# Value products of a two-layer transformer kernel in three groups of four sets a turn instead of six of two

## The chip, the cores and the metric

The kernel runs on one core of a Trainium2 chip. The metric is the device time of one execution in microseconds (us). The core has a tensor engine (PE; its weight loads are listed apart as PEld), a vector engine (DVE), a scalar engine (ACT), GpSimd (POOL) and SyncE (SP), which issues the DMAs. Each runs its own list of instructions in order, and they wait for each other by semaphores.

## The reference

Two transformer layers, each with attention and a feed-forward part on the same normalized input, over a batch of 2 sequences of 1024 rows and 512 columns, all in float32. Cut to what matters here:

```python
x = L0_attn_X                                  # (2, 1024, 512)
xn = _layernorm(x, axis=-1)
x = x + _L0_attn_ref(xn, ...) + _L0_ffn_ref(xn, ...)
xn = _layernorm(x, axis=-1)
x = x + _L1_attn_ref(xn, ...) + _L1_ffn_ref(xn, ...)

# attention: 16 heads of 32 columns, rotary embedding, causal mask
scores = jnp.einsum('bhqd,bhkd->bhqk', Qr, Kr) * DH ** (-0.5)
scores = jnp.where(causal, jnp.finfo(scores.dtype).min, scores)
pattern = jax.nn.softmax(scores, axis=-1)
heads = jnp.einsum('bhqk,bhkd->bqhd', pattern, Vh).reshape(b, t, d)
return heads @ Wo.T

# feed-forward: hidden 2048 in layer 0, 1408 in layer 1 (there with scales for rows)
gated = jax.nn.silu(gate) * up
return jnp.einsum('bsh,dh->bsd', gated, w_down)
```

## The kernel before

The program is one list of steps, `STEPS`, made by Python functions before anything is emitted. Every engine walks the whole list and emits its own part of each step, so the list sets the order on all five engines at once. There are four parts of it: two sequences times two layers (`layer(b, l)`, by `plan` and `paced`).

A part has four **turns**, one for each group of four heads. A turn consists of

- 32 **natural** steps (`nat`): scores in natural order, in which the vector engine finds the row maxima and the scalar engine sums exponentials, to get the logarithm of each softmax denominator (`guess`, `better`, `log`, `flip` put it into rows of `QS`);
- 12 **sets** of the transposed scores (`SETS`; 4 for the first half of the query rows, 8 for the second), each of four `st` steps, one a head: a matmul of up to 512 columns into one of three PSUM banks (`SS` two, `OE` one), and an exponential by the scalar engine into the tile `pr`, from which the value product reads. In the sets on the diagonal (0 to 3 and 8 to 11) GpSimd masks a block (`causal`) when the four exponentials are done;
- the **value products** (`pv`), one a set: for each of the four heads a matmul whose stationary operand is 32 columns of `val` and which writes its own 32 partitions of the bank `O` (half of `OE`). Four heads thus take four strips of 32 columns of the array;
- `heads` (the scalar engine copies `O` to `ah`, the vector engine makes the rest `al`), then four output products (`wo`, three matmuls each) that the vector engine adds to `xres`;
- at the end the next turn's four **projections** (`proj`, 12 matmuls each), merged with the output products of this turn by `merge`.

`pr` holds the weights of `RING` = 4 sets. The first exponential of set i waits for the value product of set i - 4 (semaphore `p_pv`, in `st_` of the scalar engine). The same tile holds the rotary halves of the projections (`parts`, `swapped`), so the vector engine's part of a projection must come behind the value products that read there.

`weighted` places the value products before: behind the last `st` of sets 2, 4, 6, 8 and 10 the two sets (i - 2, i - 1), and sets 10 and 11 at the end of the turn, where `merge` puts them between the first and the second projection.

The feed-forward part is cut in pieces of four matmuls (`G` gate, `U` up; three pieces each a chunk and half) and the down products (`D`), and these are the filling: `PACE` has one digit for each item of the attention, the number of pieces that come before it, and `LATER` delays the weight splits (`w`: the scalar engine rounds a weight to its high part, for instance `wdh`, GpSimd makes the low part). For the down weights of layer 1 GpSimd first multiplies `raw` by `ds`, and the scalar engine's cast waits for that.

All large products are three matmuls of rounded halves (high x high, high x low, low x high); the value products are plain float32, which the engine runs in two passes, so one listed instruction appears as two matmuls in the trace.

Of the kernel before, what the change touches and what calls it, by code (L numbers as in the profile page):

```python
# [52 lines left out]
SETS = [(c, kb) for c in range(NC) for kb in range(TPC * (c + 1))]  # L53
RING = 4
# [58 lines left out]
def diagonal(i):  # L113

    c, kb = SETS[i]
    return kb >= TPC * c


def weighted():

    out = []
    for i, (c, kb) in enumerate(SETS):
        out += [[("st", i, h)] for h in range(HG)]
        if diagonal(i):
            out[-1].append(("causal", i))
        for at, step in ((0, "guess"), (2, "better"), (3, "log"), (5, "flip")):
            if i == at // 2:
                out[2 * (at % 2 - 2) + 1].append((step, 1))
        if i and i % 2 == 0:
            out.append([("pv", i - 2), ("pv", i - 1)] + [("heads", SETS[i - 1][0])] * (SETS[i - 1][0] != c))  # L130
        if i == 6:
            out += output(0)
    return out
# [17 lines left out]
def projections():  # L151

    proj = [[("proj", t, False)] + [("rotate", t - 1)] * (t > 0) for t in range(2 * NC)]
    proj.append([("rotate", 2 * NC - 1)])
    return proj


def output(c):

    return [[("wo", c, i), ("add_wo", c, i)] for i in range(TPC)]  # L160
# [11 lines left out]
def turn(g, more):  # L172


    out = [[("turn", g)]]
    if more:
        out.append([("w", "A")])
    out += natural() + weighted()
    if g == NG - 1:
        return out  # L180
    n = len(SETS)
    last = [[("pv", n - 2), ("pv", n - 1), ("heads", 1)]]
    return out + merge(projections(), last + output(1))


def merge(proj, rest):

    return [proj[0], rest[0], proj[1]] + rest[1:3] + proj[2:4] + rest[3:] + proj[4:]


def plan(b, l):


    final = (b, l) == (B - 1, 1)
    gates, downs = mlp(l)
    pieces, late = in_order(gates[:-1], downs[:-1])
    items = []
    for g in range(NG):
        items += turn(g, not (final and g == NG - 1))
    if not final:  # L200
        items[items.index([("turn", NG - 1)])].insert(0, ("v_load", 1 - l))
    n = len(SETS)
    items.append([("pv", n - 2), ("pv", n - 1), ("heads", 1)] + [("v_weights", 1 - l)] * (not final))
    items += output(1)
    if l == 1 and not final:
        halves = [k for k, it in enumerate(items) if ("pv", TPC * 2 - 1) in it]
        items[halves[-1]].append(("x_next", 0))
        items[-TPC - 1].append(("x_next", 1))
        for rt in range(TPC):
            items[rt - TPC].append(("row", 0, rt))  # L210
        items[-1] += normal(0)

    (g0, g1), (d0, d1) = gates[-1], downs[-1]
    if final:
        g0[-1] = [x for x in g0[-1] if x[0] != "w"]
        g1, d1 = ([[x for x in p if x[0] != "w"] for p in q] for q in (g1, d1))
    pieces += g0[:3] + late + g0[3:] + g1[:3]
    if l == 0:
        rows = [piece + [("row", 1, rt)] for rt, piece in enumerate(d0)]
        rows[-1] += normal(1)  # L220
        pieces += rows + g1[3:] + early(1) + [piece + [("row", 1, TPC + i)] for i, piece in enumerate(d1)]
        items += norms(1, range(TPC))
    else:
        for c, d in enumerate((d0, d1)):
            for i, piece in enumerate(d):
                piece.append(("store", c * TPC + i))
        pieces += d0 + g1[3:9]
        if not final:
            items += norms(0, range(TPC))
            pieces[-1].append(("keep", 0))  # L230
        pieces += g1[9:] + (early(0) if not final else []) + d1
    first = opening(l)
    if (b, l) != (0, 0):
        first = [x for x in first if [x] not in early(l)]
    else:
        first.insert(first.index(("rotate", 1)) + 1, ("first",))
        first.append(("second",))
    return first, items, pieces
# [7 lines left out]
def normal(layer):  # L246

    return [("stats", layer, 0), ("xn", layer, 0), ("xn", layer, 1)]


def layer(b, l):

    first, items, pieces = plan(b, l)
    return loads(first + paced(items, pieces, PACE[b][l], LATER[b][l]))

# [13 lines left out]
def opening(layer):  # L269
# [13 lines left out]

PACE = (
    (
        ("30010030010010010003030201121212022010111001000101100100000101000001000010100000010200000100000000101",
         "00000210010100102003020311132121112010011021000000010100101101000000000100100000011010000201000000110",
         "30000101000101010112121211120212121021010100100000201000001001000001001001010000010011000000000000100",
         "040001011002010110130302020212120210200100110000010100200101010000010000101000000100100000117037j040"),
        ("01002201010101021022053203121111111020002001000000100000000000000000000000000000000000000000000000003",  # L290
         "00000021000101010113021212111113020210020101000001001000000100100002000000100000000000000000000000022",
         "00100011010001020112030303021112121030100101000002001000000101000000000000000000000000000000000000010",
         "0101000200000200011210202011101101010101000000000010000000000000000000000000000000000000000010015040"),
    ),
    (
        ("40001110100001100203020311121203111011010100200000200100000103000000000010100000100100000010000000012",
         "00000110101010013102101111211121111020120001000010010102001001000000000100100001002100000100000000011",
         "30000111000101010103120322021121212021001001000000100100000101000001000010100000010120000010000000001",
         "003000110110100210130302021112120220100101110000020010001010010000010000100100000100100001018027j220"),
        ("13001111000100110302050311210121111100100001000100100200001001000000000000000000000000000000000000001",  # L300
         "10200011000100101013122112111112210210021001000000100100000100100000000010010000000000000000000000201",
         "00100210020101010112030302120212121020111001000001000000000101000000000000000000000000000000000000030",
         "0000111000102000102111430301010100000000000000000000000000000000000000000000000000000000000d000"),
    ),
)
LATER = (("04410342c042070023000200", "111ic009o00023l200"),
         ("0090030dk0201f4011000200", "511400087042265"))
STEPS = START + [x for b in range(B) for l in (0, 1) for x in [("begin", b, l)] + layer(b, l)]


# [867 lines left out]
```

## Time and profile before

| | |
|---|---|
| median of 3 runs | 1912.29 us (1911.0 to 1917.44) |
| profiled execution, its own time | 1915.39 us |
| its span | 1913.7 us |
| mean granted TensorE clock | 0.988 |
| PE busy | 1806.6 us, 94% |
| ACT busy | 1091.3 us, 57% |
| DVE busy | 1049.8 us, 55% |
| POOL busy | 721.5 us, 38% |

The span is the time from the first to the last instruction of the profiled execution. A busy share is an average over stretches with different limits: the tensor engine's matmuls are pipelined, each is listed for longer (0.39 us for 512 columns) than it keeps the next one away (0.23 us), so its busy time says that something was in the array, and the starts of neighbouring matmuls say what each really costs.

### The profile page before, as it was taken

The numbers are of one execution on the slowest core, as the hardware profiler recorded it, in microseconds if no ns is written. First come the engines' busy times: TensorE is split into PE (matmuls) and PEld (weight loads), VectorE is DVE, ScalarE is ACT, GpSimd is POOL, SyncE is SP. The second block draws the span as 40 slices with busy tenths as digits, with TensorE's granted clock in tenths as the row PEclk, the third lists the DMA queues.
The fourth block names the chain that finished last, engine by engine and source line by source line (L and its number), as shares of the span: only waits on it lengthen the run. The fifth ranks groups of instructions, "written<-read, shape, count | busy, mean of one in ns | idle before, by whom it ended". The sixth has DMA issues, their size and how long they took to land.

```text
span 1913.7 us, 24678 instructions
## 1 busy us (share of the span) xinstructions
PE 1806.6 (94%) x8656; PEld 1328.4 (69%) x8656; DVE 1049.8 (55%) x2368; ACT 1091.3 (57%) x2445; POOL 721.5 (38%) x628
## 2 busy tenths in 40 slices
PE   5899999999999999998899999999999999998988
PEld 4677767777777576766487677777777767776655
DVE  5455557473456373837357374655536646555453
ACT  2575747575246574757536566565732575756463
POOL 2335343433333443514324252535343425343331
PEclk9999999999999999999999999999999999999989
DMA  6213132130131221304152040314111213121201
GB/s 209 77 46 85 45 78 60 48 104 30 58 94 45 52 76 31 101 9 127 37 179 78 23 111 28 83 46 127 46 55 50 77 35 94 41 76 40 66 13 44
DMA packets 66314, 130.32 MB, mean 68 GB/s; under 512 B 7696, under 2 KB 8720, under 8 KB 65168
## 3 DMA queue, kind: packets, MB, share of 16 engines
q1 hardware_dynamic: 66192, 128.75, 23.3%
q8 instruction: 69, 1.13, 0.3%
q14 instruction: 53, 0.43, 0.1%
HBM read 73.67 MB, written 4.19 MB: 41 GB/s over the span
## 4 chain that ended last, share of the span: by engine, by line
PE 77%; DVE 9%; ACT 8%; issue 3%; POOL 2%; DMA 1%; PEldq 0%; SPq 0%; DVEq 0%; ACTq 0%; POOLq 0%
PE D L984 17%; PE G L984 12%; PE U L984 12%; PE OE L984 8%; PE OE L1082 7%; PE SS L1066 6%; PE SS L984 5%; PE OE L1045 3%; PE OE L1066 3%; PE SS L1045 3%; DVE xres L946 2%; ACT OE L669 2%; ACT SS L669 2%; ACT pr L688 1%; DVE OE L904 1%
## 5 line engine op out<-in xcount | busy, mean ns | idle before, releaser
L946 DVE TENSOR_TENSOR xres<-D,xres 128x512 f32<-128x512 f32 x352 | 239.2, 689 | 262.7 <-PE D L984 259.4
L688 ACT ACTIVATE pr<-SS 128x512 f32<-128x512 f32 (+3 forms) x512 | 234.6, 499 | 110.7 <-PE SS L1066 109.3
L782 POOL TENSOR_TENSOR hl<-tt,hh 128x512 fp32r<-128x512 f32 x108 | 139.9, 1296 | 378.6 <-ACT hh L706 378.4
L669 ACT ACTIVATE OE<-OE,mp 128x384 f32<-128x384 f32 (+3 forms) x256 | 204.1, 798 | 84.0 <-DVE mp L904 83.1
L904 DVE CUSTOM_DVE_ANT_0 OE<-OE,mask 128x384 f32<-128x384 f32 (+3 forms) x256 | 221.0, 873 | 56.2 <-PE OE L1045 54.8
L800 POOL TENSOR_SCALAR_AFFINE_SELECT pr<-pr 128x512 f32<-128x512 f32 x128 | 81.3, 638 | 313.1 <-ACT pr L688 313.1
L904 DVE CUSTOM_DVE_ANT_0 SS<-SS,mask 128x128 f32<-128x128 f32 (+3 forms) x256 | 170.3, 675 | 39.2 <-PE SS L1045 38.5
L984 PE MATMUL G<-xh,wgh 128*128 128x512 f32 x432 | 175.4, 406 | 15.8 <-DVE tt L957 12.3
L669 ACT ACTIVATE SS<-SS,mp 128x128 f32<-128x128 f32 (+3 forms) x256 | 162.4, 635 | 48.1 <-DVE mp L904 46.9
L1066 PE MATMUL SS<-QS,KS 98*128 98x512 f32 (+2 forms) x512 | 169.3, 379 | 13.4 <-ACT pr L688 8.4
L984 PE MATMUL D<-wdh,hh 128*128 128x512 f32 x432 | 170.8, 395 | 1.2 <-issue 0.8
L984 PE MATMUL G<-xl,wgh 128*128 128x512 f32 x432 | 171.7, 397 | 0.0
L984 PE MATMUL G<-xh,wgl 128*128 128x512 f32 x432 | 171.6, 397 | 0.0
L984 PE MATMUL U<-xl,wuh 128*128 128x512 f32 x432 | 171.2, 396 | 0.0
L984 PE MATMUL U<-xh,wuh 128*128 128x512 f32 x432 | 170.8, 395 | 0.0
L984 PE MATMUL U<-xh,wul 128*128 128x512 f32 x432 | 170.4, 394 | 0.0
L984 PE MATMUL D<-wdl,hh 128*128 128x512 f32 x432 | 169.2, 392 | 0.0
L984 PE MATMUL D<-wdh,hl 128*128 128x512 f32 x432 | 169.0, 391 | 0.0
L706 ACT CAST hh<-tt 128x512 fp32r<-128x512 f32 x108 | 67.2, 622 | 162.8 <-DVE tt L960 162.3
L1082 PE MATMUL OE<-pr,val 128*32 128x512 f32 (+3 forms) x1536 | 147.4, 501 | 1.0 <-POOL pr L800 1.0
L688 ACT ACTIVATE pr<-OE 128x512 f32<-128x512 f32 (+3 forms) x256 | 125.7, 491 | 38.8 <-PE OE L1066 37.3
L1066 PEld LDWEIGHTS SS<-QS,KS 98*128 98x128 f32 x512 | 93.9, 190 | 77.4 <-ACT pr L688 48.4
(121 smaller groups left out, 3713.3 us busy)
## 6 DMA issues: line engine op xcount, KB each, us to landing
KS<-pr SPq DMA_DIRECT2D x128, 192.0 KB, 3.3
QS<-pr SPq DMA_DIRECT2D x128, 192.0 KB, 3.3
raw<-in_wgate_dram SPq DMA_DIRECT2D x28, 512.0 KB, 3.7
raw<-in_wup_dram SPq DMA_DIRECT2D x28, 512.0 KB, 3.7
raw<-in_wdown_dram SPq DMA_DIRECT2D x27, 512.0 KB, 3.7
raw<-in_wqk_dram SPq DMA_DIRECT2D x16, 512.0 KB, 3.5
trig<-in_rope_dram SPq DMA_DIRECT2D x4, 1024.0 KB, 5.1
xres<-in_x_dram SPq DMA_DIRECT2D x4, 1024.0 KB, 6.6
```

Of the source, the lines that this page charges most:

```text
L669: act.activation(s, s, ACT.Exp, bias=mp[:, c, at:at + 1], scale=-1.0, accum_out=se[:, c, at:at + 1]) \
L688: act.activation(weights(i)[:, h, skip:W], SB[(i * HG + h) % 3][:, skip:W], ACT.Exp, scale=-1.0) \
L706: act.copy(hh[:, fc, :], tt[:, (blk * nfc + fc) % 2, :]).then_inc(sem["a_hh"], 1)
L782: pool.tensor_tensor(hl[:, fc, :], tt[:, (blk * nfc + fc) % 2, :], hh[:, fc, :].bitcast(F32), ALU.subtract) \
L800: pool.affine_select(out=blocks, in_=blocks, pattern=[[0, HG], [1, P]], compare_op=ALU.is_ge, fill=0.0, base=0, channel_multiplier=-1).the ...
L904: dve.tensor_tensor_reduce(s, s, mask[:, NC * W - w_:NC * W], 1.0, 3e38, ALU.add, ALU.min, mp[:, c, at:at + 1]) \
L946: dve.tensor_tensor(xres[:, rt, :], d[:, :], xres[:, rt, :], ALU.add).then_inc(sem["v_dfree"], 1)
L984: ins = pe.matmul(dst, a, b_, start=i == 0, stop=i == len(seq) - 1)
L1045: ins = pe.matmul(s[:, part * W:part * W + wide], QS[0:STACK, c, h, qb * P:(qb + 1) * P], KS[0:STACK, h, part * W:part * W + wide], start= ...
L1066: pe.matmul(SB[k % 3][:, first:W], KS[0:SHIFT, h, kb * P:(kb + 1) * P], QS[0:SHIFT, c, h, first:W], start=True, stop=True).then_inc(sem["p ...
L1082: ins = pe.matmul(O[h * DH:(h + 1) * DH, skip:W], val[:, kb, (n.turns * HG + h) * DH:(n.turns * HG + h + 1) * DH], weights(i)[:, h, skip:W ...
```

## The change

The value products come in groups of `RING` = 4 sets: in `weighted` the sets i - 4 to i - 1 for i = 4 and 8, put before the last `st` of set i (`out.insert(len(out) - 1, ...)`) rather than behind it, and sets 8 to 11 at the end of the turn (`last_heads`). `merge` puts this last group ahead of the first projection instead of between the first two. `PACE` and `LATER` are new numbers throughout. No instruction's size or kind is changed, and no arithmetic.

```diff
@@ weighted
-        if i and i % 2 == 0:
-            out.append([("pv", i - 2), ("pv", i - 1)] + [("heads", SETS[i - 1][0])] * (SETS[i - 1][0] != c))
+        if i and i % RING == 0:
+            out.insert(len(out) - 1, [("pv", k) for k in range(i - RING, i)] + [("heads", SETS[i - 1][0])] * (SETS[i - 1][0] != c))
@@ turn
-    n = len(SETS)
-    last = [[("pv", n - 2), ("pv", n - 1), ("heads", 1)]]
-    return out + merge(projections(), last + output(1))
+    return out + merge(projections(), [last_heads()] + output(1))
+
+
+def last_heads():
+
+    n = len(SETS)
+    return [("pv", k) for k in range(n - RING, n)] + [("heads", 1)]
@@ merge
-    return [proj[0], rest[0], proj[1]] + rest[1:3] + proj[2:4] + rest[3:] + proj[4:]
+    return [rest[0], proj[0], proj[1]] + rest[1:3] + proj[2:4] + rest[3:] + proj[4:]
@@ plan
-    n = len(SETS)
-    items.append([("pv", n - 2), ("pv", n - 1), ("heads", 1)] + [("v_weights", 1 - l)] * (not final))
+    items.append(last_heads() + [("v_weights", 1 - l)] * (not final))
@@ PACE, LATER (all rows are new; one of each)
-        ("01002201010101021022053203121111111020002001000000100000000000000000000000000000000000000000000000003",
+        ("01003100110010102032053212121111101010010001000200100000000010000000000000000000000000000000000003",
...
-LATER = (("04410342c042070023000200", "111ic009o00023l200"),
-         ("0090030dk0201f4011000200", "511400087042265"))
+LATER = (("02r0000l0040ap002o010100", "0102900dx02024E100"),
+         ("02a0224mj0200ba02p000100", "0100b00ba000078"))
```

**Place 1, the tensor engine in the third turn of layer 1 (first sequence), sets 7 to 10.** `SS<-QS,KS` and `OE<-QS,KS` are score products (`st`), `OE<-pr,val` with 32x512 x8 are the value products of two sets of full width. Before:

```order
L1066 MATMUL SS<-QS,KS 128x512 x2
L1066 MATMUL OE<-QS,KS 128x512
L1066 MATMUL SS<-QS,KS 128x512 x2
L1066 MATMUL OE<-QS,KS 128x512
L1082 MATMUL OE<-pr,val 32x512 x8
L1066 MATMUL SS<-QS,KS 128x384 x2
L1066 MATMUL OE<-QS,KS 128x384
L1066 MATMUL SS<-QS,KS 128x384
L1066 MATMUL SS<-QS,KS 128x256
L1066 MATMUL OE<-QS,KS 128x256
L1066 MATMUL SS<-QS,KS 128x256 x2
L1082 MATMUL OE<-pr,val 32x512 x4
```

Two sets of value products stand behind set 8, and the next group begins behind set 10. The same place now:

```order
L1069 MATMUL SS<-QS,KS 128x512
L1069 MATMUL OE<-QS,KS 128x512
L1069 MATMUL SS<-QS,KS 128x512 x2
L1085 MATMUL OE<-pr,val 32x512 x16
L1069 MATMUL OE<-QS,KS 128x512
L1069 MATMUL SS<-QS,KS 128x384 x2
L1069 MATMUL OE<-QS,KS 128x384
L1069 MATMUL SS<-QS,KS 128x384
L1069 MATMUL SS<-QS,KS 128x256
L1069 MATMUL OE<-QS,KS 128x256
```

Sets 4 to 7 are one group of 16 instructions, ahead of the last score product of set 8, and no value product follows until the score products of the turn are done.

**Place 2, the tensor engine at the end of the same turn.** `SS<-xh,wqkh` and the like are matmuls of a projection. Before:

```order
L984 MATMUL SS<-xh,wqkl 128x512
L984 MATMUL SS<-xh,wqkh 128x512
L984 MATMUL SS<-xl,wqkh 128x512
L984 MATMUL SS<-xh,wqkl 128x512
L1082 MATMUL OE<-pr,val 32x256 x4
L1082 MATMUL OE<-pr,val 32x128 x4
L984 MATMUL SS<-xh,wqkh 128x512
L984 MATMUL SS<-xl,wqkh 128x512
L984 MATMUL SS<-xh,wqkl 128x512
```

The last group (sets 10 and 11) stood between the first and the second projection. Now:

```order
L1069 MATMUL OE<-QS,KS 128x256
L1069 MATMUL SS<-QS,KS 128x256 x2
L1069 MATMUL OE<-QS,KS 128x256
L1085 MATMUL OE<-pr,val 32x512 x4
L1085 MATMUL OE<-pr,val 32x384 x4
L1085 MATMUL OE<-pr,val 32x256 x4
L1085 MATMUL OE<-pr,val 32x128 x4
L987 MATMUL SS<-xh,wqkh 128x512
L987 MATMUL SS<-xl,wqkh 128x512
L987 MATMUL SS<-xh,wqkl 128x512
```

The group has sets 8 to 11 and follows the last score product directly; both projections come behind it.

**Place 3, the scalar engine at the end of the second turn of layer 1 (first sequence).** `pr<-SS` and `pr<-OE` are exponentials, `wdh<-raw` the cast of a scaled down weight, `ah<-OE` the cast of the heads. Before:

```order
L688 ACTIVATE pr<-OE 128x384
L688 ACTIVATE pr<-SS 128x384
L688 ACTIVATE pr<-SS 128x256
L709 CAST wdh<-raw 128x1024
L688 ACTIVATE pr<-OE 128x256
L688 ACTIVATE pr<-SS 128x256 x2
L688 ACTIVATE pr<-OE 128x128
L688 ACTIVATE pr<-SS 128x128 x2
L688 ACTIVATE pr<-OE 128x128
L694 CAST ah<-OE 128x512
```

Seven exponentials of the turn stand behind the cast. Now:

```order
L691 ACTIVATE pr<-SS 128x256
L691 ACTIVATE pr<-OE 128x256
L691 ACTIVATE pr<-SS 128x256 x2
L691 ACTIVATE pr<-OE 128x128
L691 ACTIVATE pr<-SS 128x128 x2
L691 ACTIVATE pr<-OE 128x128
L712 CAST wdh<-raw 128x1024
L697 CAST ah<-OE 128x512
L664 CAST pr<-pr 128x512
```

The cast has moved from among the exponentials of set 10 to behind the last one of the turn.

## Rows read from the trace of the kernel before

**Rows 1.** the page: busy shares, and the chain that ended last by engine

```profile
PE 1806.6 (94%) x8656; PEld 1328.4 (69%) x8656; DVE 1049.8 (55%) x2368; ACT 1091.3 (57%) x2445; POOL 721.5 (38%) x628
...
PE 77%; DVE 9%; ACT 8%; issue 3%; POOL 2%; DMA 1%; PEldq 0%; SPq 0%; DVEq 0%; ACTq 0%; POOLq 0%
```

**Rows 2.** windows from first to last score product, a turn of each layer

```profile
core 0: us, PE busy (x) PEld busy (x) DVE busy (x) ACT busy (x) POOL busy (x), PEclk, DMA share, GB/s
1264.90:1302.70 37.80, 37.80 (x217) 26.21 (x216) 11.25 (x23) 25.19 (x59) 10.60 (x12) 1.00 0.02 4
...
1853.50:1885.70 32.20, 30.37 (x141) 13.81 (x141) 4.96 (x13) 21.02 (x53) 4.46 (x7) 0.86 0.01 1
```

**Rows 3.** timeline, ACT: start, us busy, line, operation, [idle before it <- releaser]

```profile
843.39 1.13 ACT L688 ACTIVATE pr<-SS 128x512 f32<-128x512 f32 x2
844.35 0.67 ACT L688 ACTIVATE pr<-OE 128x512 f32<-128x512 f32 x1
846.42 0.87 ACT L688 ACTIVATE pr<-SS 128x384 f32<-128x384 f32 x2 [1.41 <-PE SS L1066]
...
850.83 0.28 ACT L688 ACTIVATE pr<-OE 128x128 f32<-128x128 f32 x1 [1.63 <-PE OE L1066]
...
851.58 0.28 ACT L688 ACTIVATE pr<-OE 128x128 f32<-128x128 f32 x1
```

**Rows 4.** groups by line, PE: the value matmuls (count, busy, mean ns, idle before)

```profile
L1082 PE MATMUL OE<-pr,val 128*32 128x512 f32 (+3 forms) x1536 | 147.4, 501 | 1.0 <-POOL pr L800 1.0
```

**Rows 5.** timeline, PEld: weight loads of one group, a round apart

```profile
844.49 0.13 PEld L1082 LDWEIGHTS OE<-pr,val 128*32 128x32 f32 x4 [0.30 <-issue]
844.91 0.13 PEld L1082 LDWEIGHTS OE<-pr,val 128*32 128x32 f32 x4 [0.30 <-issue]
```

**Rows 6.** timeline, PE, third turn of layer 1: groups and their edges

```profile
844.03 1.92 PE L1082 MATMUL OE<-pr,val 128*32 128x512 f32 x16
845.88 0.62 PE L1066 MATMUL SS<-QS,KS 98*128 98x384 f32 x2
...
851.42 0.47 PE L984 MATMUL SS<-xh,wqkh 128*128 128x512 f32 x1
...
854.03 0.39 PE L984 MATMUL SS<-xh,wqkl 128*128 128x512 f32 x1
854.35 0.86 PE L1082 MATMUL OE<-pr,val 128*32 128x256 f32 x16
855.14 0.50 PE L984 MATMUL SS<-xh,wqkh 128*128 128x512 f32 x1
855.48 0.40 PE L984 MATMUL SS<-xl,wqkh 128*128 128x512 f32 x1
855.72 0.40 PE L984 MATMUL SS<-xh,wqkl 128*128 128x512 f32 x1
```

**Rows 7.** timeline, all engines, at two down-weight casts of layer 1

```profile
746.14 2.50 POOL L775 TENSOR_TENSOR raw<-raw,ds 128x512 f32<-128x512 f32 x2
...
748.71 1.05 ACT L709 CAST wdh<-raw 128x1024 fp32r<-128x1024 f32 x1 [2.97 <-issue]
...
750.09 0.38 PE L1066 MATMUL OE<-QS,KS 98*128 98x256 f32 x1 [2.27 <-ACT pr L688]
...
921.22 0.66 PE L1066 MATMUL SS<-QS,KS 98*128 98x256 f32 x2 [2.17 <-ACT pr L688]
```

**Rows 8.** timeline, all engines, end of the last turn

```profile
1885.68 0.38 PE L1066 MATMUL OE<-QS,KS 98*128 98x256 f32 x1 [0.20 <-ACT pr L688]
...
1885.99 0.64 PE L1082 MATMUL OE<-pr,val 128*32 128x256 f32 x8
...
1886.44 0.64 POOL L800 TENSOR_SCALAR_AFFINE_SELECT pr<-pr 128x512 f32<-128x512 f32 x1 [2.03 <-ACT pr L688]
...
1887.13 0.42 PE L1082 MATMUL OE<-pr,val 128*32 128x128 f32 x8 [0.50 <-POOL pr L800]
```

More of the change, by code:

```diff
@@ L285 @@
     (
[L286 to L289, printed above, removed]
-        ("01002201010101021022053203121111111020002001000000100000000000000000000000000000000000000000000000003",
-         "00000021000101010113021212111113020210020101000001001000000100100002000000100000000000000000000000022",
-         "00100011010001020112030303021112121030100101000002001000000101000000000000000000000000000000000000010",
-         "0101000200000200011210202011101101010101000000000010000000000000000000000000000000000000000010015040"),
-    ),
@@ L295 @@
-    (
[L296 to L303, printed above, removed]
-    ),
-)
@@ L306 @@
-LATER = (("04410342c042070023000200", "111ic009o00023l200"),
-         ("0090030dk0201f4011000200", "511400087042265"))
+        ("40000120010010100102021201121212021111001100100100300000101011000000001001000010010001000000000200",
+         "00000210010010102003020321302121111101001011002010001001010101000000001000000010010011000001000111",
+         "00120011010101010112121212020212123210010010000110100000101003010000010010000000000000000000000201",
+         "01001010101110012103120201121212021101010010100010200000100010000000010100000011100200100830bf040"),
@@ new lines @@
+        ("01003100110010102032053212121111101010010001000200100000000010000000000000000000000000000000000003",
+         "00002010010010010103022212111112031011020101000011000001101001000000000000000010000000000000000002",
+         "02100020100010110023111202121112120030100100101010100000101000000000001000000000000000000000000002",
+         "0010000101000200011211020111101101001100000100000010000000000000000000000000000000000000010015040"),
+    ),
+    (
+        ("04010110110001020102020212211202111101001100111003100000101010000000000000000010010000000000000200",
+         "01021020011010020112102111211121112010010110100020100010100102000000001000000010010012000000000011",
+         "30001011000101010112120313021121212020101001000101000001001010000000010100000010020001001000000001",
+         "00301010011100111103030201121212022001001010010030000000120030000000001000000010100100100703ag220"),
+        ("50000111000102100112050302210121202010010101002010000000000010000000000000000000000000000000000003",
+         "00000201001001000113122112111112120030030010000101100000100000000000100100000000000000000000000022",
+         "00000200110110101013121203020212122011001000001100000000100010000000001000000000000000000000000012",
+         "1001010110010011101114120301010100000000000000000000000000000000000000000000000000000000d000"),
+    ),
+)
```

## The prediction

> **What bounds the kernel now.** I read the page's busy shares and its chain first: the tensor engine is busy for 94% of the span and carries 77% of the chain that ended last [rows 1]. So only what takes time out of the tensor engine's own sequence, or out of a wait in front of it, is worth anything. Next I looked at the stretches in which the value products run, because the change touches only those: a turn (one group of four heads) has 12 sets of four score products each, and from the first to the last of them the tensor engine is busy all 37.8 us in a turn of layer 0, but 30.4 of 32.2 us in the last turn of layer 1 [rows 2]. There the scalar engine makes the exponentials (one of 512 columns every 0.48 us [rows 3]) and few feed-forward matmuls are left to fill in. So there are two kinds of turn: eight of layer 0, where the tensor engine sets the pace, and eight of layer 1, where in sets 7 to 11 the exponentials do.
>
> **What a group of value products costs beyond its matmuls.** The trace has 1536 value matmuls [rows 4], 16 a group (two sets, four heads, two passes of fp32), so 96 groups: six in each of 16 turns. One group is to be read at its edges. Four matmuls on the four 32-column strips run together as one round; inside a group of two full sets a round starts 0.42 to 0.43 us after the one before it (844.49, 844.91) [rows 5]. Three excesses:
> - Entry: the full-array matmul ahead lasts 0.32 us to the group's start (854.03 to 854.35) where the plain pitch is 0.24 (855.48 to 855.72) or a little less: about 0.09 [rows 6].
> - Inside: 844.03 to 845.88 is 1.85 us for four rounds, which are 4 x 0.43 = 1.72: about 0.13. It sits at both ends (first round 0.46, the last one the rest) [rows 5, 6].
> - Exit: the first full-array matmul behind lasts 0.34 (855.14 to 855.48) in place of 0.23 to 0.24: about 0.11 [rows 6].
>
> Sum 0.33 to 0.34 us a group, whatever its size. Between the two sets of one group nothing of it is seen. The Trainium skill, TensorEngine Tiling (Array Packing), section Key Properties, says why a group should have such a price: changing the tiling mode, not only the tile, drains the engine. The trace agrees with the direction.
>
> **Term 1, the groups themselves.** Six groups become three a turn: 48 groups fewer x 0.335 = 16.1 us less on the tensor engine. In layer 0 this is worth its full half, 8 us, since nothing waits there. In layer 1 it must be looked at again, because a saved 0.33 us may become a wait for an exponential.
>
> **Term 1 in layer 1.** Before, a group of two full sets in sets 7 to 11 leaves the scalar engine idle for 1.41 us, the next for 1.63 [rows 3]: the group lasts longer than the banks of scores that stand ready. After, the group of four full sets stands behind the third score product of set 8. The first exponential of set 8 overwrites the weights of set 4, so it waits for that set's value product: 0.32 us to the group's start, two rounds of 0.43 to 0.46, some 0.3 for the signal (845.88 to 846.42 is 0.54 [rows 3, 6], less 0.23 of matmul): about 1.3 us of idle. Then three exponentials, 1.45 us, while the other three sets run (2.7 us), and the fourth score product must come round: 1.4 idle. Together 2.7, against 3.0 before: the longer group costs the scalar engine nothing more. What moves is the tensor engine's work: sets 4 and 5 go from behind set 6 into this stretch (2.2 us earlier there, less work), sets 8 and 9 leave it (1.6 us of idle less), and reappear behind the last score product (the last group is 2.2 in place of 0.8 us). Per turn: -2.2 - 1.6 + 1.6 (the fourth exponential of set 8 comes that much later) + 1.3, so about -0.9, and -0.33 for the merger of sets 0 to 3. I take the full 1.0 for these turns too; the lower bound is nothing, 8 us in all.
>
> **Term 2, the last group ahead of the first projection.** Before, 12 projection matmuls (851.42 to 854.35, 2.9 us [rows 6]) cover the last exponential and its mask; after, only value products of sets 8 to 10 do: 0.09 + 0.88 + 0.65 + 0.43 = 2.05 us before the masked set 11 is due. Is that enough? The last turn of the kernel has no projection, and shows the path bare: last score product 1885.68, mask 1886.44 to 1887.08, its value product at 1887.13, so 1.45 us [rows 8]. There and in the other final turn of layer 1 the group of two waited (1.14 us where two rounds of 256 columns are 0.43): 0.7 each, and both go: -1.4. If GpSimd is busy with a 1.3 us piece at that moment the margin of 0.6 is gone and the wait is up to 0.7; over 14 other turns that bounds the loss at 10 us, I take 0, because the new orders give no feed-forward piece behind the last score product in 15 turns. The projections themselves start later against the last score product but not against the next turn's first products: the same matmuls stand between. Heads' cast and rest now have two projections of cover instead of one before the output products: no loss.
>
> **Term 3, the scaled down-weights.** In layer 1 GpSimd multiplies these by a scale (2.50 us) and the scalar engine waits for it in order, with exponentials queued behind: 2.97 us idle at 745.7 to 748.7, and the tensor engine stands for 2.27 us; the same at 921.22, 2.17 [rows 7]. The new orders put the first cast behind the last exponential of its turn, where 7 us of value products and projections need nothing of the scalar engine, and the other behind set 6, under 12 output matmuls (2.9 us). -4.4 us. The Trainium skill, TensorE: Matmul & The Clock Gate, section Engine queue depths, has the scalar engine's queue as strictly first in, first out; the trace agrees here by the 2.97 us, and it is the rule that speaks against this change (rival 3).
>
> **Term 4, what the new filling gives back.** In the third turn of layer 0 (first batch) sets 9 to 11 have no filling now: exponentials 3.8 us (846.42 to 851.86, less the idle 1.63) [rows 3] against 1.6 us of score products: +2.2. The last turn has four feed-forward matmuls less, 0.23 each, in front of products that wait anyway: +0.9. The other pieces move by a few places; nothing in the trace prices that, and I bound it at 5 us either way.
>
> **Sum.** -16.1 - 1.4 - 4.4 + 3.1 = -18.8. The profiled execution took 1915.4 us (span 1913.7), the median of the three runs is 1912.3; 1915.4 - 18.8 = 1896.6, and against the median 1893.5. I forecast **1894**.
>
> **Rivals.**
> 1. *Only the unbound turns keep the saving* (chance 0.17): in layer 1 each 0.33 us turns into a wait for an exponential, as it would where the tensor engine is idle anyway (busy 30.4 of 32.2 us in the last turn [rows 2]). For it: two of the three terms of the layer-1 sum nearly cancel. Against: the idle of the scalar engine comes out equal. -8 - 1.4 - 4.4 + 3.1 = -10.7: 1902. The same time would come if only part of the excess is the switch. By the skill's figure for a drain through the array, 128 cycles (TensorE: Matmul & The Clock Gate, step DRAIN), at 2.4 GHz 0.05 us, two a group, it would be an estimated 5 us of the 16; the measured edges say 0.33, and the measurement decides.
> 2. *More comes* (0.12): the four-set groups let the scalar engine catch up and the pauses of layer 1 shrink by another 1 us a turn: 1886.
> 3. *The hold takes over, slower* (0.07): the place is the first exponential of sets 4 and 8, held until the first value product of its group is done. Held with it are tanh, casts and splits behind it in order. If the 1.3 + 1.4 us at set 8 and some 1.4 at set 4 are not offset by the idle of the old groups, eight turns of layer 1 pay 4.1 each, 33 us, less 16: 1929. It decides from 2.0 us a turn on. Against: the old gaps, 1.41 and 1.63, are there and vanish. A further price would be the clock: in the last turn the mean granted clock is 0.86 already [rows 2].
> 4. *The orders eat it* (0.14): the mergers save what they should, but pieces moved by the new table wait at their new places, 5 us more than my bound, and terms 2 and 3 do not come: 1908 to 1914.
>
> **How the numbers follow.** Forecast and its neighbourhood 0.50. The range takes in rivals 1 and 2: 1884 to 1908; outside lie rival 3, most of rival 4. Faster by more than 0.3% (0.3% is about what a measurement of this kernel can tell from no change) means below 1906.5: 0.50 + 0.17 + 0.12 and a little of rival 4, 0.80. Within 0.3%: 0.13. Slower: 0.07.
>
> **What would show it.** Right: 48 groups of value matmuls; a group of four full sets 3.57 us (8 x 0.43 + 0.13) and a diagonal one 2.3; the same 0.09 and 0.11 at the edges; scalar idle of about 1.3 and 1.4 at the four-set group of layer 1; no 2.2 us wait beside a down-weight cast in the second and last turn of layer 1, first batch. Wrong: value groups longer than 3.6 us, waits inside the last group for the mask, score products behind a group that wait for longer than one exponential, or wider gaps in the first, natural-order score stretches, where the new filling is all that changes.

## The result, and the profile after

The changed kernel takes 1899.57 us (median of four runs, 1899.04 to 1901.31) beside 1914.87 us for the kernel before on the same chip (1911.0 to 1918.65). The ratio is 0.9922, with a 95% interval of 0.9897 to 0.9947: 15 us faster. The forecast was 1894, the range 1884 to 1908. The time is in the range; the reasons, as shown below, are mostly not the ones of the sum. Each experiment below has its own ratio to the kernel before, run beside it on one chip (medians 1913.7 to 1916.1 us); where two changed kernels are compared by their times, they may have run on different chips, and the ratios are the safer guide.

The profiled execution took 1899.04 us (span 1897.3), against 1915.39 (span 1913.7) before. Its page, busy shares and chain, beside [rows 1]:

```profile
PE 1801.1 (95%) x8656; PEld 1335.4 (70%) x8656; DVE 1051.5 (55%) x2368; ACT 1093.5 (58%) x2445; POOL 720.5 (38%) x628
...
PE 77%; DVE 9%; ACT 8%; issue 3%; POOL 2%; DMA 0%; PEldq 0%; SPq 0%; DVEq 0%; ACTq 0%; POOLq 0%
```

PE's busy time fell by 5.5 us only, while the span fell by 16.4: two thirds of the gain is waiting that is gone. The two windows of [rows 2], from the first to the last score product of the same two turns, and the value matmuls of [rows 4]:

```profile
1254.20:1290.30 36.10, 35.88 (x197) 25.39 (x196) 10.80 (x22) 24.41 (x56) 8.40 (x10) 1.00 0.01 1
...
1835.60:1868.50 32.90, 29.47 (x124) 14.68 (x125) 4.96 (x13) 21.31 (x52) 4.01 (x7) 0.79 0.01 1
```

```profile
L1085 PE MATMUL OE<-pr,val 128*32 128x512 f32 (+3 forms) x1536 | 140.5, 507 | 0.3 <-POOL pr L803 0.2
```

The groups are what was foretold. PE in a turn of layer 1 (third turn, first sequence), the group of four full sets, then the diagonal one, answering to [rows 6]:

```profile
834.26 3.64 PE L1085 MATMUL OE<-pr,val 128*32 128x512 f32 x32
837.83 0.50 PE L1069 MATMUL OE<-QS,KS 98*128 98x512 f32 x1
...
842.23 2.36 PE L1085 MATMUL OE<-pr,val 128*32 128x512 f32 x32
844.52 0.50 PE L987 MATMUL SS<-xh,wqkh 128*128 128x512 f32 x1
844.86 0.39 PE L987 MATMUL SS<-xl,wqkh 128*128 128x512 f32 x1
845.09 0.40 PE L987 MATMUL SS<-xh,wqkl 128*128 128x512 f32 x1
```

From start to start, 3.57 us (3.57 foretold) and 2.29 (2.3), the exit again 0.34 in place of 0.23. The scalar engine at the same group, answering to [rows 3]:

```profile
835.39 0.60 ACT L691 ACTIVATE pr<-OE 128x512 f32<-128x512 f32 x1 [1.61 <-PE OE L1085]
...
838.37 0.60 ACT L691 ACTIVATE pr<-OE 128x512 f32<-128x512 f32 x1 [1.40 <-PE OE L1069]
```

It stands 1.61 and 1.40 us (1.3 and 1.4 foretold). And all engines at the down-weight cast of the second turn of layer 1, answering to [rows 7]:

```profile
743.33 2.52 POOL L778 TENSOR_TENSOR raw<-raw,ds 128x512 f32<-128x512 f32 x2
...
745.92 1.05 ACT L712 CAST wdh<-raw 128x1024 fp32r<-128x1024 f32 x1 [3.27 <-POOL raw L778]
746.06 0.39 PE L987 MATMUL SS<-xh,wqkh 128*128 128x512 f32 x1
```

The scalar engine still waits for GpSimd's product, now for 3.27 us, but the cast is behind the last exponential, and PE goes on with projections: no bracket stands behind its row.

**Where the time went, by part.** A part runs from its first natural score product to that of the next part, so a piece of its neighbour's work is in it; the last one ends with PE's last row. In us, from the starts of the PE rows:

| | layer 0, seq. 1 | layer 1, seq. 1 | layer 0, seq. 2 | layer 1, seq. 2 |
|---|---|---|---|---|
| before | 492.1 | 451.5 | 490.0 | 408.0 |
| after | 492.5 | 443.2 | 491.7 | 399.3 |

Layer 0 gained nothing and lost 2.1 us; layer 1 gained 17.0; the remaining 1.3 us lie ahead of the first part. Each number is from one execution. In the five traces that have the old layer 0 (before, layer 1 only, early multiply alone, and the two mixtures below) its two parts take 980.9 to 983.8 us together, in the three that have the new one (after, layer 0 only, change with early multiply) 983.2 to 984.5, so the loss is rather 1 to 2 us. The prediction had 8 us for the merged groups in layer 0 alone, "in full".

### The profile page after: what moved, and what is told of

Same layout as the page of the kernel before. It is cut to its first block, busy times and chain, and to the rows that moved or that the text cites. A ratio compares the mean times of both kernels' runs of the same rounds, so it can differ in the third digit from the quotient of the medians.

```text
span 1897.3 us, 24679 instructions
## 1 busy us (share of the span) xinstructions
PE 1801.1 (95%) x8656; PEld 1335.4 (70%) x8656; DVE 1051.5 (55%) x2368; ACT 1093.5 (58%) x2445; POOL 720.5 (38%) x628
## 4 chain that ended last, share of the span: by engine, by line
PE 77%; DVE 9%; ACT 8%; issue 3%; POOL 2%; DMA 0%; PEldq 0%; SPq 0%; DVEq 0%; ACTq 0%; POOLq 0%
PE D L987 17%; PE G L987 12%; PE U L987 12%; PE OE L987 8%; PE OE L1085 7%; PE SS L1069 6%; PE SS L987 5%; PE OE L1048 3%; PE OE L1069 3%; PE SS L1048 3%; DVE xres L949 2%; ACT OE L672 2%; ACT pr L691 2%; ACT SS L672 2%; DVE OE L907 2%
## 5 line engine op out<-in xcount | busy, mean ns | idle before, releaser
L691 ACT ACTIVATE pr<-SS 128x512 f32<-128x512 f32 (+3 forms) x512 | 238.5, 500 | 89.2 <-PE SS L1069 59.4
L1069 PE MATMUL SS<-QS,KS 98*128 98x512 f32 (+2 forms) x512 | 177.2, 387 | 11.5 <-ACT pr L691 5.2
L664 ACT CAST pr<-pr 128x512 fp32r<-128x512 f32 x64 | 39.8, 622 | 185.3 <-DVE pr L897 133.4
L791 POOL TENSOR_TENSOR pr<-pr,trig 128x512 f32<-128x512 f32 x64 | 96.5, 1508 | 126.1 <-DVE pr L888 126.1
```

The costliest lines, as they stand in the source:

```text
L691: act.activation(weights(i)[:, h, skip:W], SB[(i * HG + h) % 3][:, skip:W], ACT.Exp, scale=-1.0) \
L791: pool.tensor_tensor(sw, sw, trig[:, 1, t // 2 * W:(t // 2 + 1) * W], ALU.mult).then_inc(sem["g_sin"], 1)
L1069: pe.matmul(SB[k % 3][:, first:W], KS[0:SHIFT, h, kb * P:(kb + 1) * P], QS[0:SHIFT, c, h, first:W], start=True, stop=True).then_inc(sem["p ...
```

## The experiments

### One layer at a time

The tables and the grouping of the changed kernel in layer 0 only (`FOUR = (0,)`), and in layer 1 only (`(1,)`); the other layer as before.

```diff
-        if i and i % RING == 0:
+        if l not in FOUR and i and i % 2 == 0:
+            out.append([("pv", i - 2), ("pv", i - 1)] + [("heads", SETS[i - 1][0])] * (SETS[i - 1][0] != c))
+        if l in FOUR and i and i % RING == 0:
```

> Groups of four sets, the new end of a turn and the new numbers of the filling in the two layer-0 parts only; layer 1 as in the kernel before. The theory of the prediction (in layer 0 nothing waits, each saved switch counts): 8.0 us less by 24 groups, 2.2 given back, so about 6 us faster. The theory formed from the trace of the changed kernel (in layer 0 the saving is eaten by waits of score products for exponentials, 12.5 us more of them): within 1.5 us of before.

> The same in the two layer-1 parts only; layer 0 as in the kernel before. The theory of the prediction: 8.0 for 24 groups, 1.4 for the two bare last groups, 4.4 for two down-weight casts, 0.9 given back: about 13 us faster. The theory from the trace: all of the gain, 15 to 17 us, is here.

Measured: layer 0 only 1921.02 us, ratio 1.0025 (1.001 to 1.004); layer 1 only 1900.59, 0.9926 (0.9903 to 0.9948). The whole gain is layer 1's. Layer 0 only is some 5 us slower than before, outside both forecasts, and most of that isn't made in layer 0: in its trace the two layer-0 parts are 1.0 us longer than before, and the two layer-1 parts, whose order is the old one, 2.8 us longer, with 45 us at the lower of the two granted clocks in place of 31. In layer 0 the edit is worth nothing or a little less.

### The scaled down weights alone

Layer 1 is also where GpSimd multiplies the down weights by a scale. Of the casts of `wdh` with PE standing behind them [rows 7] has two; over the whole trace of before there are three more, here from timelines of all engines:

```profile
595.90 1.05 ACT L709 CAST wdh<-raw 128x1024 fp32r<-128x1024 f32 x1 [3.90 <-POOL raw L775]
...
597.89 0.73 PE L1045 MATMUL OE<-KS,QS 96*128 96x512 f32 x2 [3.65 <-ACT OE L669]
...
1747.64 1.04 ACT L709 CAST wdh<-raw 128x1024 fp32r<-128x1024 f32 x1 [3.91 <-POOL raw L775]
...
1749.63 1.03 PE L1045 MATMUL OE<-KS,QS 96*128 96x512 f32 x2 [3.92 <-ACT OE L669]
...
1844.40 1.05 ACT L709 CAST wdh<-raw 128x1024 fp32r<-128x1024 f32 x1 [1.82 <-issue]
...
1846.49 1.01 PE L1045 MATMUL SS<-KS,QS 96*128 96x512 f32 x2 [2.21 <-ACT SS L669]
```

These stand in the natural score stretches (L1045), with natural exponentials (L669) queued behind the cast. Five waits: 3.65 + 2.27 + 2.17 + 3.92 + 2.21 = 14.2 us. The experiment takes only them away, in the kernel before: GpSimd's multiply becomes a step of its own, up to 16 steps ahead of the cast. Groups, filling and the orders of the other four engines are untouched.

```diff
+        if p in put:                      # p: place of the cast, put: 16 steps ahead of it or less
+            out.append(("scale", "D"))
...
-            def w(n, kind):
+            def scale(n, kind):
                 slot = SLOT[kind]
                 if n.scaled(slot):
                     pool.wait_ge(sem[f"raw{slot}"], n(f"raw{slot}", 16))
```

> The kernel before, with GpSimd's multiplication of the layer-1 down weights by their scales put up to 16 steps of the list ahead of the cast that waits for it; nothing else moved. It takes away what makes the scalar engine wait. Theory of the prediction: two waits go, 4.4 us. Theory from the trace: five such waits (3.8, 2.3, 2.2, 4.1 and 2.4 us, 14.8 together) stand in the kernel before, so 9 to 14 us go. Rival (the waits only move to the next exponential or to GpSimd's other work): under 3 us.

Measured: 1898.82 us, ratio 0.9915 (0.9892 to 0.9937), 16.6 us, a little over the 9 to 14 expected. **In time, this alone is as good as the whole change.** Part of it is the clock: its six runs have a mean granted clock of 0.992, the 17 of before beside them 0.988 (what that is worth stands in the last section). All engines at two of the five places (first and second turn of layer 1):

```profile
584.74 2.52 POOL L794 TENSOR_TENSOR raw<-raw,ds 128x512 f32<-128x512 f32 x2
...
591.65 1.04 ACT L728 CAST wdh<-raw 128x1024 fp32r<-128x1024 f32 x1
...
741.91 1.08 ACT L728 CAST wdh<-raw 128x1024 fp32r<-128x1024 f32 x1
742.43 1.71 PE L1104 MATMUL OE<-pr,val 128*32 128x512 f32 x16
744.07 0.38 PE L1088 MATMUL OE<-QS,KS 98*128 98x256 f32 x1
```

No bracket on the cast and none on PE. Since PE's 8656 matmuls are the same in the same order, the two traces can be laid over each other, matmul by matmul. The lead of the new one grows by 1.9 us round 597, 2.4 round 750, 2.4 round 921, 5.6 round 1749 and 2.5 round 1846, 14.8 in all. What moves elsewhere (1 to 3 us up or down at some ten places) goes with the granted clock and nearly cancels: the lead at the end is 13.8.

### The same on top of the change

The same edit on the changed kernel.

> The changed kernel with the same early scaling of the layer-1 down weights as in the third experiment. Its trace has one wait of the scalar engine for a scaled weight left (3.3 us, 1.8 of it on the tensor engine). If the change and the early scaling remove the same waits: 1 to 3 us faster than the changed kernel, 1897 to 1899. If they were independent gains (15 and 16 us): 1884.

Measured: 1899.99 us beside 1913.72 for before, 0.9928 (0.9915 to 0.9941), where the changed kernel has 0.9922. It adds nothing, not even the 1 to 3 us expected: the new orders had already taken PE out of these waits. So the two ways to remove them are exchangeable, and what else the change does nets, in time, to about zero.

### Groups without the new filling, and the new filling without groups

First the groups of four and the new end of the turn, with the old tables carried over item by item.

> Groups of four and the new end of a turn, but the old filling: each item of the attention keeps its old number of feed-forward pieces, the numbers of the old group items go to the item that follows, the weight splits keep their old delays. If the mergers alone bring the gain: 16 us less, plus 1.4. If the longer groups make score products wait where no filling was moved for them (theory from the trace): between 10 us faster and 5 us slower. Rival of the hold (33 us in layer 1): over 10 us slower.

Measured: 1946.52 us, 1.0167 (1.0143 to 1.0191), 31 us slower than before. Of the three forecasts only that of the hold (over 10 us slower) allows it, which is why the hold gets an experiment of its own below. Then the new tables with six groups of two.

```diff
-            out.insert(len(out) - 1, [("pv", k) for k in range(i - RING, i)] + ...
+            out.insert(len(out) - 1, [("pv", i - 2), ("pv", i - 1)] + ...
+        elif i and i % 2 == 0:
+            out[-1] += [("pv", i - 2), ("pv", i - 1)]
...
-    return [("pv", k) for k in range(n - RING, n)] + [("heads", 1)]
+    return [("pv", k) for k in range(n - 2, n)] + [("heads", 1)]
```

> The changed kernel with its new filling, but the value products again in six groups of two sets, at the old places (behind sets 2, 6 and 10, and at the new places of sets 4, 8 and the end of the turn). Switches alone (0.335 us each, 48 more): 16 us slower than the changed kernel. If value products behind sets 2, 6 and 10 are also cover for the exponentials, waits before the score products of sets 3, 7 and 11 (20 us in the changed kernel's layer 0 and 1) shrink: only 2 to 10 us slower.

Measured: 1923.76 us, 1.0053 (1.0039 to 1.0068), 24 us slower than the change: outside both forecasts, since neither priced the new end of a turn for groups of two. 48 switches are 16 us; about 12 more is waiting inside the last group for the mask, since two sets ahead of the first projection don't cover it. In the view of who waited for GpSimd's mask, PE has in this kernel

```profile
  PE OE L1087: 12.2, 19
```

that is 12.2 us in 19 waits, against 1.0 in 2 before and 0.2 in 1 after. Counted from the starts of the PE rows, the waits before score products shrink against the changed kernel by 4 us only (82 to 77), not by anything near the 20 that stood there: with the new filling the groups behind sets 2, 6 and 10 are little missed.

The slow one is the more telling. PE's waits by releaser, with us, count and the longest, first before and then with fours and the old filling (whose L1047 and L669 are the lines L1066 and L688 of before):

```profile
PEld SS L1066 <- ACT pr L688: 48.4, 107, 2.9
...
PE SS L1066 <- ACT pr L688: 8.4, 23, 2.2
```

```profile
PEld SS L1047 <- ACT pr L669: 56.6, 131, 4.0
...
PE SS L1047 <- ACT pr L669: 21.8, 32, 3.8
```

On these rows PE waits for 13.4 us more and the weight loads for 8.2; one wait can stand in both rows, so the two don't add up. Summed from the starts of the PE rows (what lies between two score products beyond 0.23 us for 512 columns, value groups left out), by layer:

| waits before score products, us | before | after | fours, old filling |
|---|---|---|---|
| layer 0, all sets | 8.2 | 20.7 | 32.5 |
| layer 0, set 3 | 0.8 | 2.8 | 8.4 |
| layer 0, set 11 | 0.6 | 3.1 | 8.9 |
| layer 1, all sets | 53.6 | 62.5 | 79.1 |

Sets 3 and 11 stand where the groups behind sets 2 and 10 have gone. Those groups were not only an expense of 0.33 us: 0.8 to 1.9 us of value products there gave the scalar engine time for its exponentials. Take them away and PE arrives at the next score product too early. The row of layer 0 shows the change's balance in this layer: 24 switches fewer are 8.0 us, 12.5 us of waits came; the natural stretches and the ends of the turns, counted the same way, are 3 us shorter, which brings the sum to within a microsecond of the 2.1 us lost. The row of layer 1 is softer than that of layer 0: with the pitch taken as 0.443 ns a column for every width, layer 0 comes out the same within 0.4 us (8.6, 20.8, 32.5), layer 1 as 55.6, 60.8 and 75.5. And in layer 1 the row of before holds the two cast waits of [rows 7], 4.4 us, which are gone after.

### Is it the hold of the ring?

Rival 3 put the waits down to `pr` holding only four sets. The slow kernel once more, with room for five; to find the space, the low parts of the gate and up weights share the tiles of the high parts, so the feed-forward products are computed from wrong low parts, at the same sizes and counts.

```diff
-RING = 4
+RING = 5
+GROUP = 4
...
-wgh, wgl = sb("wgh", [P, 2, KC, P], F32R), sb("wgl", [P, 2, KC, P], F32R)
+wgh = wgl = sb("wgh", [P, 2, KC, P], F32R)
```

> The fourth experiment's kernel (groups of four, old filling, 31 us slower than before) with room for five sets of weights instead of four, so the first exponentials of sets 4 and 8 need not wait for the group's first value product. To make room the low parts of the gate and up weights share the tiles of the high parts, so the feed-forward products get wrong second operands; instructions, sizes and waits stay. If the hold makes the loss: 15 us or more of the 31 come back. If the missing cover behind sets 2, 6 and 10 makes it: under 8 us come back.

Measured: 1942.61 us, 1.0149 (1.0132 to 1.0166). The fifth set returns 2 to 4 us of the 31 (3.9 by the two times, 3.4 by the ratios, 2.2 by each one's distance from before on its own chip), and the waits by set stay (layer 0 30.4 us, layer 1 80.2). The hold is there and small; the missing cover is the main part.

### The price of a group, by cutting it

The changed kernel with the groups at sets 4 and 8 each cut in two by one score product: 32 groups more, nothing else moved.

```diff
-            out.insert(len(out) - 1, [("pv", k) for k in range(i - RING, i)] + ...
+            out.insert(len(out) - 1, [("pv", i - 4), ("pv", i - 3)])
+            out[-1] += [("pv", i - 2), ("pv", i - 1)] + ...
```

> The changed kernel, with the groups at sets 4 and 8 cut in two by the one score product that stood behind them: two sets ahead of it, two behind. 32 more groups, everything else the same. Switches alone: 10.7 us slower. If the length of a group starves the scalar engine (1.61 and 1.40 us idle at such a group), the score product comes 1.6 to 1.9 us earlier and layer 1 gets back up to 1 us a group: 0 to 5 us slower.

Measured: 1903.04 us, 0.9945 (0.9932 to 0.9958), 3.5 us above the change and not 10.7. By part against after: +3.3, -0.9, +1.6, -0.2. In layer 0, 16 groups cost 4.9 us, **0.31 each**, near the 0.335 of the edges; in layer 1 nothing is left of the price. Two things take it away there. The waits at sets 5 and 9 of layer 1, right behind the cuts, shrink from 10.6 to 5.8 us (counted with the pitch by columns), as the expectation has it. And the clock helps: this trace spends 27 us at the lower clock and the changed kernel's 41, with 3.4 of the 13.7 us between them in layer 0 and 10.2 in layer 1. By the estimate of the last section the kernel would be some 8.6 us above the change at an equal clock, so the 3.5 us must not be read as the price of 32 groups. PE at one cut, layer 0:

```profile
143.58 1.92 PE L1086 MATMUL OE<-pr,val 128*32 128x512 f32 x16
145.44 0.49 PE L1070 MATMUL OE<-QS,KS 98*128 98x512 f32 x1
145.86 1.49 PE L1086 MATMUL OE<-pr,val 128*32 128x512 f32 x12
```

1.86 us for four rounds (4 x 0.43 + 0.14), then 0.42 for a score product whose pitch is 0.23: 0.33 for the extra group.

### The new end alone

The kernel with the early multiply and groups of two, and the last group moved ahead of the first projection.

```diff
-    return [proj[0], rest[0], proj[1]] + rest[1:3] + proj[2:4] + rest[3:] + proj[4:]
+    return [rest[0], proj[0], proj[1]] + rest[1:3] + proj[2:4] + rest[3:] + proj[4:]
```

> The kernel before with the early scaling (1898.8 us in the third experiment), and of the change only one part: the last group (two sets) ahead of the first projection instead of behind it. The 12 matmuls that covered the last mask then stand behind it. Expected of the bare path in the last turn (the value product of set 11 comes no sooner than 1.45 us after the last score product, two rounds of 256 columns hide 0.43 of it): 0.7 to 1.0 us in each of 14 turns, 10 to 14 us slower than the third experiment. Rival (the projection was no cover, the wait is short because the exponentials are ahead): under 4 us.

Measured: 1910.48 us, 0.997 (0.995 to 0.9989), 11.7 us slower than the same kernel without the swap (10.5 by the ratios). All engines at one of the 14 places:

```profile
850.25 0.38 PE L1088 MATMUL OE<-QS,KS 98*128 98x256 f32 x1 [0.19 <-ACT pr L707]
850.57 0.64 PE L1104 MATMUL OE<-pr,val 128*32 128x256 f32 x8
851.02 0.63 POOL L822 TENSOR_SCALAR_AFFINE_SELECT pr<-pr 128x512 f32<-128x512 f32 x1 [2.03 <-ACT pr L707]
851.71 0.43 PE L1104 MATMUL OE<-pr,val 128*32 128x128 f32 x8 [0.50 <-POOL pr L822]
```

So the move costs with two sets what [rows 8] show, 0.7 to 0.8 us a turn, and with four sets next to nothing: sets 8 to 10 are the cover. In the changed kernel a mask is late at two places only; this is one:

```profile
1190.13 0.64 POOL L803 TENSOR_SCALAR_AFFINE_SELECT pr<-pr 128x512 f32<-128x512 f32 x1
...
1190.82 0.43 PE L1085 MATMUL OE<-pr,val 128*32 128x128 f32 x8 [0.17 <-POOL pr L803]
```

### Best of both

By part, layer 1 of the first sequence looked better with fours (443.2 us against 449.6 with the early multiply alone), the others better with groups of two. Two mixtures, both with the early multiply: fours in layer 1 of the first sequence only, and fours in layer 1 of both.

```diff
-FOUR = (1,)
+FOUR = ((0, 1),)
```

> A version meant to beat both: groups of four with their new filling only in layer 1 of the first sequence, groups of two with the old filling in the other three parts, and the early scaling everywhere. Taken from the lengths of the parts in the traces so far (layer 0: 492.0 and 488.9, layer 1: 441 to 443 with groups of four and 399.4 with groups of two and early scaling, against 492.5, 491.7, 443.2 and 399.3 in the changed kernel): 3 to 5 us faster than the changed kernel, 1895 to 1897. If the parts' lengths are only scatter of the clock's falls: within 1.5 us of 1899.

> Groups of four with their new filling in both layer-1 parts, groups of two with the old filling in layer 0, early scaling everywhere. Beside the second experiment (1900.6 us) it tells whether the groups of four gain anything in layer 1 once the casts' waits are gone: against the third experiment (groups of two everywhere, 1898.8 us) only the layer-1 groups differ. Switches alone: 8 us faster than that, 1891. If the waits of the score products eat it there too: 1897 to 1901.

Measured: 1897.63 us (1894.85 to 1901.69), 0.9908 (0.9888 to 0.9929), and 1898.35, 0.9916 (0.9896 to 0.9935). Neither is told apart from the change, nor from the early multiply alone (0.9922 and 0.9915). The gains seen by part don't add up, since a part's length also depends on where the clock falls (last section): the 449.6 us hold 17 us at the lower clock, the 443.2 us 7, and the profiled execution of the early multiply was the slowest of its six (1901.62 us).

## Why the prediction came near, and where its steps failed

**What bounds the kernel.** Held. PE carries 77% of the chain before and after. But "in layer 0 the tensor engine sets the pace" was read from its busy time alone, and was used for a conclusion that it doesn't carry (next but one).

**The price of a group.** Held: 0.33 us at the edges, 3.57 us for the group of four, 0.31 each by cutting. The drain when the tiling mode changes, as the Trainium skill has it (TensorEngine Tiling (Array Packing), section Key Properties), agrees with this.

**Term 1, -16.1 us.** The step that failed: "In layer 0 this is worth its full half, 8 us, since nothing waits there". Measured +2.1 us over both parts of layer 0. The switches did go; what was not counted is that nothing waited there because the old groups were in the right places. The busy share of a stretch holds for its order. The sum counted the excess of the groups behind sets 2, 6 and 10, and never asked who used the 0.8 to 1.9 us that they last: the exponentials. 12.5 us of new waits ate the 8. With the old filling the loss would have been 31 us; the new tables bring the feed-forward pieces to these places and so buy back most of it, which is their work in this change and not the "3.1 us given back" of term 4. In layer 1 the lower bound, nothing, was the true one or near it: the waits before score products grow by 5 to 9 us although two of the cast waits (4.4 us) left them, so 10 to 13 us of new waits stand against the 8 of the switches. Of the 17.0 us won there 14.8 is what the five cast waits were worth by themselves, and the natural stretches, whose filling is new too, are some 5 us shorter beyond that. Rival 1 was right on layer 1, where the saving became waits, and wrong on layer 0: it let the unbound turns keep theirs.

**Term 1, the scalar engine at set 8.** Held in its own numbers, 1.61 and 1.40 us. The waits that decide are elsewhere, behind sets 2 and 10.

**Term 2, -1.4 us.** Right for the four-set group, and its bound of 10 us for the case that cover lacks is what it costs with two sets (10.5 to 11.7). Two new mask waits, 0.37 and 0.30 us from start to start, are what it gave back.

**Term 3, -4.4 us.** The mechanism was right, the size a third: five places and 14.2 us instead of two and 4.4. I looked for waits only in the stretches that the diff touches, the score products of the sets; the three others stand in the natural stretches, which the new tables change as well. A view of all of the scalar engine's waits for `raw`, over the whole trace, would have shown them.

**Term 4, +3.1 us.** Not separable as stated; the row of layer 0 in the table of waits stands in its place.

**The sum.** -18.8 foretold, -16.4 in the profiled executions and -15.3 in the medians. Term 1 was some 16 us too large, term 3 some 10 too small, and term 4 (3.1) falls away, since its cost is already in the balance of term 1: -18.8 + 16 - 10 - 3 = -16. Two errors of opposite sign came out near the time, which is luck; as an explanation the sum was wrong in its largest term.

**Rivals.** 2 did not come. 3 was priced at 33 us by the hold; the hold alone is worth 2 to 4 us, but a loss of just that size exists, by the other mechanism and with the old filling. 4 named the right kind of thing (moved pieces wait at their places) and missed that the same new order also takes waits away.

**What stays open.** Whether the merged groups leave something in layer 1. The kernels with and without them there (early multiply in both) lie within 2 us of each other in time. But in their profiled executions the early multiply alone has layer-1 parts of 849.0 us and the change with early multiply 843.3, each with 34 us at the lower clock, while over all runs the first had the higher clock (0.992 against 0.9885). So 3 to 6 us may be there that the clock takes back; each part's length is from one execution, and no run separates the two.

## What to carry to other kernels

Before an instruction group is moved or merged for its overhead, ask what its duration covers: time taken from a busy engine is only a gain if the engine that feeds it is ahead at that place. Where an engine's queue holds a cast that waits for a slow producer, list all such waits over the whole trace before costing a new order, and try the cheap repair first (the producer a few steps earlier): here it gave as much time as new groups and tables for the whole kernel. And test the terms of a sum one by one even when the total fits, since two large errors can cancel.

## What the runs showed of the hardware

**The clock falls in the middle of work, at the price of whole terms of the sum.** PE in the changed kernel, the last group of the first turn of layer 1, the same instructions as at 842.23 above:

```profile
641.40 4.01 PE L1085 MATMUL OE<-pr,val 128*32 128x512 f32 x32
645.34 0.50 PE L987 MATMUL SS<-xh,wqkh 128*128 128x512 f32 x1
```

3.94 us in place of 2.29. The windows ahead of it and at it (PE busy, PEld, DVE, ACT, POOL, granted clock, DMA):

```profile
637.00:641.40 4.40, 4.06 (x17) 2.35 (x13) 0.00 (x0) 3.85 (x12) 1.79 (x3) 1.00 0.00 0
640.70:645.50 4.80, 4.80 (x36) 1.97 (x37) 0.00 (x0) 1.08 (x5) 1.27 (x2) 0.64 0.00 0
```

A mean of 0.64 of 2.4 GHz: most of the window at the lower level, 1.2 GHz. Ahead of it PE was listed as busy for 4.06 of 4.40 us at the full clock, with score products that came at the pace of the exponentials (13 of them, of 512, 384 and 256 columns, which at their pitches of 0.23, 0.17 and 0.12 us would take 1.9 us; the longest idle time in front of one was 0.34). In the kernel with the early multiply, soon after one of the removed waits, the clock falls again where before it did not:

```profile
925.00:935.00 10.00, 9.63 (x40) 4.27 (x36) 2.77 (x4) 4.03 (x8) 0.64 (x1) 0.84 0.01 2
```

There the 2.4 us won at 921 were lost again (3.1) within 20 us. Over the profiled execution the time at the lower level is 44 us before, 41 after, 37.5 with the early multiply, 51 with layer 1 only, 55 with layer 0 only, 79 with fours and the old filling and 27 with the cut groups. What it costs can be read from runs of one and the same kernel: over all runs here, a run whose mean granted clock is 0.001 lower is about 1.2 us longer (a straight line through each kernel's runs, one slope for all). With this estimate the kernels at an equal clock of 0.990 would take 1913 us before, 1898 after, 1901 with the early multiply, 1898 with both, and 1907 with the cut groups. Orders that differ little thus differ by some 10 us of lower clock and by 2 to 5 us of time, and a difference of that size between two kernels here is no proof of a saved wait or switch.

**A group of value products costs about 0.33 us over its rounds by its edges** (0.31 each where 16 were added in layer 0), with two sets and with four, and four sets in one group show nothing between them (3.57 us = 8 x 0.43 + 0.13).
